# A graph network's second table stored as a float32r part and an exact rest, and summed with one float32r product a tile

## The reference, cut to what matters

```python
for l in range(2):
    W = jnp.einsum('rb,bio->rio', coeffs[l], bases[l])     # 8 relations, 256 x 256 each
    h = jnp.einsum('ni,rio->rno', x, W)                    # the table: node x relation -> 256 numbers
    msg = h[edge_type, src] * deg_inv[dst][:, None]        # one row of the table per edge
    agg = jax.ops.segment_sum(msg, dst, num_segments=6250)
    x_new = agg + x @ self_loops[l]
    x = relu(x_new) if l == 0 else x_new
# then: x_in + x + attention(xn), and experts on its layernorm
```

## Time and profile before

| | us |
|---|---|
| median of 3 runs | 2587.59 |
| lowest and highest run | 2583.8, 2588.66 |
| span of the profiled execution, first to last instruction | 3411.3 |
| POOL busy, idle before its gathers (profiled) | 1649.4, 1418.2 |
| PE busy, DVE busy, ACT busy (profiled) | 2398.6, 1074.1, 626.8 |

### The profile page before, as it was taken

The page is one execution under the profiler, slowest core; times in us unless marked ns, Lnnn a source line. Parts: engine busy times, 40 slices in busy tenths (PEclk is TensorE's granted clock), DMA queues, the critical chain, the costliest instruction groups (busy, mean ns, idle before and its releaser), DMA issues. The chain is left out here.

```text
span 3411.3 us, 37691 instructions
## 1 busy us (share of the span) xinstructions
PE 2398.6 (70%) x9525; PEld 1737.8 (51%) x9528; DVE 1074.1 (31%) x3125; ACT 626.8 (18%) x1391; POOL 1649.4 (48%) x1712
## 2 busy tenths in 40 slices
PE   6999357777777777776882766666666666566287
PEld 3788235555555555554561544444444444455065
DVE  3787022222222222222220333333233333234233
ACT  4455101111111111110120011111111211110033
POOL 0000655555555555555506555555655555551645
PEclk9999678888888888888895877777777777788587
DMA  8764433334333333433423332333332223231531
GB/s 225 250 232 192 139 100 123 128 125 133 123 124 124 126 124 125 128 122 112 131 90 93 88 91 87 88 87 88 91 88 84 86 87 90 85 87 32 164 110 54
DMA packets 159887, 397.24 MB, mean 116 GB/s; under 512 B 34926, under 2 KB 92241, under 8 KB 145932
## 3 DMA queue, kind: packets, MB, share of 16 engines
q0 software_dynamic: 81648, 219.65, 22.1%
q10 hardware_dynamic: 35772, 124.12, 9.4%
q1 hardware_dynamic: 42337, 51.93, 5.5%
HBM read 260.70 MB, written 138.94 MB: 117 GB/s over the span
## 5 line engine op out<-in xcount | busy, mean ns | idle before, releaser
L515 POOL DMA_INDIRECT gnn_ring<-table,g_idx x1564 | 1512.7, 967 | 1418.2 <-PE gnn_pagg L558 680.0
L558 PE MATMUL gnn_pagg<-gnn_ring,gnn_oh 128*128 x3904 | 1215.4, 460 | 483.7 <-issue 427.0
L558 PEld LDWEIGHTS gnn_pagg<-gnn_ring,gnn_oh 128*128 128x128 f32 x3904 | 838.0, 228 | 886.9 <-issue 759.7
L542 DVE TENSOR_TENSOR gnn_oh<-gnn_col,g_dst 128x256 f32<-128x256 f32 x976 | 408.9, 426 | 1471.2 <-DVEq L49 1214.0
L800 ACT COPY second_wr<-gnn_pm 128x512 f32<-128x512 f32 x196 | 103.0, 597 | 1107.8 <-DMA pre_bs<-in_L_gnn_bases 992.7
L1054 ACT ACTIVATE gnn_qe<-gnn_pq,gnn_bq 128x128 f32<-128x128 f32 x98 | 36.1, 368 | 1078.0 <-remote 1036.1
L402 PE MATMUL pre_psum<-pre_whigh,pre_high 128*128 128x512 f32 x392 | 159.0, 406 | 13.1 <-DVE pre_low L309 8.1
L336 DVE SCALAR_TENSOR_TENSOR second_wr<-pre_bs,pre_cr,second_wr 128x512 f32<-128x512 f32 x232 | 159.5, 748 | 2.8
L744 PE MATMUL gnn_pm<-gnn_whigh,gnn_high 128*128 128x512 f32 x392 | 157.5, 402 | 3.5 <-issue 2.5
L744 PE MATMUL gnn_pm<-gnn_whigh,gnn_low 128*128 128x512 f32 x392 | 153.8, 392 | 6.8 <-issue 6.7
L744 PE MATMUL gnn_pm<-gnn_wlow,gnn_high 128*128 128x512 f32 x392 | 152.9, 390 | 4.2 <-issue 4.2
(11 more groups left out here) (174 smaller groups left out, 2382.6 us busy)
## 6 DMA issues: line engine op xcount, KB each, us to landing
table<-pre_rows ACTq DMA_DIRECT2D x49, 1024.0 KB
table<-second_wr ACTq DMA_DIRECT2D x48, 1024.0 KB
gnn_ring<-table,g_idx POOLq DMA_INDIRECT x1564
bucket<-gnn_zrow SPq DMA_DIRECT2D x16, 650.0 KB
g_xT<-bucket SPq DMA_DIRECT2D x20, 520.0 KB, 6.3
pre_bs<-in_L_gnn_bases SPq DMA_DIRECT2D x32, 240.0 KB
pre_bs<-in_L_gnn_bases SPq DMA_DIRECT2D x30, 256.0 KB
x1T<-gnn_x1T ACTq DMA_DIRECT2D x49, 128.0 KB
```

Source lines behind the costliest of these rows:

```text
L515: eng.indirect_dma_start(self.ring[:, q % RG, t, 0:D], None, self.g.table[self.l][:, :], bass.IndirectOffsetOnAxis(ap=self.g.idx[:, at:at ...
L542: self.nc.vector.tensor_tensor(self.oh[:, h, :, :], self.col[:, :].unsqueeze(1).to_broadcast([P, n, P]), self.g.dst[:, ds(q * TPG + h * n, ...
L558: mm = nc.tensor.matmul(pagg[:, k, 0:self.width], self.oh[:, h, i, :], self.ring[:, ds(q & (RG - 1), 1), t, 0:self.width].rearrange("p o n ...
```

## The change

The second layer's table gets rows of 512 numbers (2 KB): the float32r part of the 256 numbers and, behind it, the rest (number minus part), which is stored as float32r as well. The second layer's sum multiplies such a row by a float32r matrix of ones and zeros, 512 columns in one product, and the two halves of the result are added afterwards. The ring of the second layer has 8 groups in place of 16, of 2 KB rows. In the first layer ACT's copy of a chunk writes the float32r part, DVE makes the rest of each chunk (`rows_low`, at the end of its step), and the block is stored with four DMAs of 512 KB, each after its rest is there; the buffer of a chunk is single. TensorE's next `multiply` waits for the four rests.

```diff
-RG = 16
+RG = (16, 8)
...
-        self.table = [dram(f"table{l}", (NP * R, D), F32) for l in range(2)]
+        self.table = [dram(f"table{l}", (NP * R, (1 + l) * D), F32) for l in range(2)]
...
+        self.rg = RG[l]
+        self.row = D if l == 0 else 2 * D
-        self.width = D + 1 if l == 0 else D
-        self.ring = s.sb("ring", [P, RG, TPG, ROW])
+        self.width = D + 1 if l == 0 else 2 * D
+        self.ring = s.sb("ring", [P, self.rg, TPG, ROW if l == 0 else 2 * D])
-        self.oh = s.sb("oh", [P, HALF, TPG // HALF, P])
+        self.oh = s.sb("oh", [P, HALF, TPG // HALF, P], F32 if l == 0 else F32R)
+        self.tiles = self.ring if l == 0 else self.ring[:, :, :, :].bitcast(F32R)
...
-                eng.indirect_dma_start(self.ring[:, q % RG, t, 0:D], None, self.g.table[self.l][:, :],
+                eng.indirect_dma_start(self.ring[:, q % rg, t, 0:self.row], None, self.g.table[self.l][:, :],
...
                     mm = nc.tensor.matmul(pagg[:, k, 0:self.width], self.oh[:, h, i, :],
-                                          self.ring[:, ds(q & (RG - 1), 1), t, 0:self.width].rearrange("p o n -> p (o n)"),
+                                          self.tiles[:, ds(q & (self.rg - 1), 1), t, 0:self.width].rearrange("p o n -> p (o n)"),
...
-        rows = wr
+        rows = wr[:, :, :].rearrange("p a (n r i d) -> p (a n) r i d", n=NC // 2, r=R // NC, i=2)
...
+            def rows_low():
+                for n in range(NC):
+                    reach(eng, hi_ok)
+                    V.tensor_tensor(rows[:, n, :, 1, :].bitcast(F32R), pm[:, n, 0:CW].rearrange("p (r d) -> p r d", d=D),
+                                    rows[:, n, :, 0, :], ALU.subtract).then_inc(lo_ok, 1)
+
             def step(b, k, prev):
                 agg.onehots(eng, b, seq)
...
                 front(k)
                 if b == NB - 1:
                     low_part(k)
+                if prev:
+                    rows_low()
...
             keys((NB - 1) % 2)
+            rows_low()
...
                 if b:
-                    eng.wait_ge(rows_ok, b)
+                    eng.wait_ge(lo_ok, NC * b)
...
-            def store(b, k):
-                reach(eng, stored[k], 16)
+            def store(b):
                 for n in range(NC):
+                    reach(eng, stored[n], 16)
                     reach(eng, chunk_ok)
-                    ins = nc.scalar.copy(rows[:, k, n * CW:(n + 1) * CW], pm[:, n, 0:CW])
-                    if b == NB - 1 and n == NC // 2 - 1:
-                        ins.then_inc(half_ok, 1)
-                        reach(eng, half_ok)
-                        eng.dma_start(table_rows(g, 1, b)[:, 0:R * D // 2], rows[:, k, 0:R * D // 2]).then_inc(stored[k], 16)
-                ins.then_inc(rows_ok, 1)
-                reach(eng, rows_ok)
-                lo = R * D // 2 if b == NB - 1 else 0
-                eng.dma_start(table_rows(g, 1, b)[:, lo:], rows[:, k, lo:]).then_inc(stored[k], 16)
+                    nc.scalar.copy(rows[:, n, :, 0, :].bitcast(F32R),
+                                   pm[:, n, 0:CW].rearrange("p (r d) -> p r d", d=D)).then_inc(hi_ok, 1)
+                for n in range(NC):
+                    reach(eng, lo_ok)
+                    eng.dma_start(table_rows(g, 1, b)[:, n * 2 * CW:(n + 1) * 2 * CW],
+                                  rows[:, n, :, :, :].rearrange("p r i d -> p (r i d)")).then_inc(stored[n], 16)
...
-                    ins = V.tensor_tensor(xb[:, j, :], xb[:, j, :], bo[:, :], ALU.add)
+                    V.scalar_tensor_tensor(out=xb[:, j, :], in0=agg.pagg[:, j, 0:D], scalar=g.dinv[:, ds(n - 1, 1)],
+                                           in1=xb[:, j, :], op0=ALU.mult, op1=ALU.add)
+                    ins = V.scalar_tensor_tensor(out=xl[:, :], in0=agg.pagg[:, j, D:2 * D], scalar=g.dinv[:, ds(n - 1, 1)],
+                                                 in1=bo[:, :], op0=ALU.mult, op1=ALU.add)
...
-                    ins = V.scalar_tensor_tensor(out=xb[:, j, :], in0=agg.pagg[:, j, 0:D], scalar=g.dinv[:, ds(n - 1, 1)],
-                                                 in1=xb[:, j, :], op0=ALU.mult, op1=ALU.add)
+                    eng.sem_inc(agg.agg_free, 1)
+                    ins = V.tensor_tensor(xb[:, j, :], xb[:, j, :], xl[:, :], ALU.add)
```

More of the change, by code:

```diff
@@ L29 @@
 NTP = NG * TPG
-RG = 16
+RG = (16, 8)
+REUSED = NG - min(RG)
 FREE = 2
@@ L85, in __init__ @@
         self.bound = s.sb("bound", [1, P], I32)
-        self.reuse = s.sb("reuse", [1, NG - RG], I32)
+        self.reuse = s.sb("reuse", [1, REUSED], I32)
         self.iota = s.sb("iota", [P, P])
@@ L160, in startup @@
         bni = s.sb("bni", [P, NB + 1], I32)
-        uio = s.sb("uio", [1, NG - RG], I32)
-        ush = s.sb("ush", [1, NG - RG], I32)
+        uio = s.sb("uio", [1, REUSED], I32)
+        ush = s.sb("ush", [1, REUSED], I32)
         idi = s.sb("idi", [P, P], I32)
@@ L488, in __init__ @@
         self.groups_in, self.gate, self.ring_ok = sems["groups_in"], sems["gate"], sems["ring_ok"]
-        self.landed = [s.sem(f"landed{j}") for j in range(RG)]
+        self.landed = [s.sem(f"landed{j}") for j in range(self.rg)]
         self.agg_ok, self.agg_free = sems["agg_ok"], sems["agg_free"]
@@ L499, in count @@
     def count(self, eng, between=None):
+        rg = self.rg
         for q in range(NG):
-            eng.wait_ge(self.landed[q % RG], 16 * sum(min(TPG, NT - p * TPG) for p in range(q % RG, q + 1, RG)))
+            eng.wait_ge(self.landed[q % rg], 16 * sum(min(TPG, NT - p * TPG) for p in range(q % rg, q + 1, rg)))
             eng.sem_inc(self.groups_in, 1)
@@ L507, in gather @@
     def gather(self, eng):
+        rg = self.rg
         for q in range(NG):
-            if q >= RG and q % FREE == 0:
-                last = eng.value_load(self.g.reuse[0:1, q + FREE - 1 - RG:q + FREE - RG], min_val=2, max_val=NG + NB)
+            if q >= rg and q % FREE == 0:
+                last = eng.value_load(self.g.reuse[0:1, q + FREE - 1 - rg:q + FREE - rg], min_val=2, max_val=NG + NB)
                 eng.wait_ge(self.pairs, last)
@@ L524, in begin @@
         if self.l == 0:
-            for j in range(RG):
+            for j in range(self.rg):
                 ins = self.nc.vector.memset(self.ring[:, j, :, D:ROW], 1.0)
@@ L602, in gnn_first @@
         xn_ok, xT_ps, high_ok, low_ok, split_ok = (s.sem(n) for n in ("xn_ok", "xT_ps", "high_ok", "low_ok", "split_ok"))
-        chunk_ok, half_ok, rows_ok = (s.sem(n) for n in ("chunk_ok", "half_ok", "rows_ok"))
+        chunk_ok, hi_ok, lo_ok = (s.sem(n) for n in ("chunk_ok", "hi_ok", "lo_ok"))
         p_ok, p_free, kt_ok, er_ok, kf_ok, kv_done = (s.sem(n) for n in (
@@ L607, in gnn_first @@
         kept = [s.sem(f"kept{k}") for k in range(2)]
-        stored = [s.sem(f"stored{k}") for k in range(2)]
+        stored = [s.sem(f"stored{n}") for n in range(NC)]
         dve_own = g.dve_own
@@ L821, in step @@
                 if prev:
-                    store(b - 1, 1 - k)
+                    store(b - 1)
                 reach(eng, kt_ok)
@@ L825, in step @@
                 nc.scalar.activation(kr[:, k, :], kt[:, k, :], ACT.Relu).then_inc(er_ok, 1)
+            for n in range(NC):
+                eng.sem_inc(stored[n], 16)
             for k in range(2):
-                eng.sem_inc(stored[k], 16)
                 eng.sem_inc(kept[k], 16)
@@ L833, in _ @@
                 step(b, b % 2, b > 0)
-            store(NB - 1, (NB - 1) % 2)
+            store(NB - 1)
+            for n in range(NC):
+                reach(eng, stored[n], 16)
             for k in range(2):
-                reach(eng, stored[k], 32 if k == (NB - 1) % 2 else 16)
                 reach(eng, kept[k], 16)
@@ L852, in gnn_second @@
         xb = s.sb("xb", [P, 2, D])
+        xl = s.sb("xl", [P, D])
         xf = s.sb("xf", [P, 2, D])
```

7 lines of the change are left out of this document (3 added, 4 removed).

## The result

The kernel before takes 2587.49 us (4 runs, 2583.8 to 2588.66), the changed one 2752.45 us (4 runs, 2749.94 to 2758.38): **slower by 165 us, ratio 1.0648, 95% interval 1.0633 to 1.0664**. It lies in the range, 42 us above the predicted 2710. The profiled execution of the changed kernel took 2749.94 us, with a span of 2748.2, so that its rows show the time of a plain run.

A forecast was written before the change was run, and what follows sets the result against it. The prediction took POOL's gathers to set the pace of both layers. Late rests 62, clock 53 and first layer's end 7 made 122 us on the median of 2587.6: 2710 us, range 2635 to 2760 us.

The forecast's parts named there:

- What bounds the kernel: Both layers: POOL's gathers, 1.267 us each, set the pace; the stretches sum to 2591 us against a median of 2587.6.
- The second layer at nothing: Second layer's sum: TensorE saves 293 us, none on the path, since POOL still issues 782 gathers; cost nothing.
- the 2 KB rows at nothing: Second layer's gathers: 2 KB rows may take the same 0.95 us, DMA share 0.40 to 0.80; no cost.
- The rests: First layer: subtractions delay the next one-hot matrices, sum 2.45 us late in 47 steps, 115 us less 53: 62 us.
- slack: First layer: TensorE alone needs 962 us, POOL's way 1014 us, leaving 53 us, 1.1 us a block.
- then 0.55 us idle: First layer, DVE: idle time put between the fourth subtraction's end and the one-hot comparison column, 0.55 us.
- The clock: First layer, TensorE: the clock falls after the wait in two blocks of three, 1.7 us each: 53 us.
- every block: Rival for the first layer: the clock falls in every block, 80 us, total 2737 us; chance 0.18.
- The first layer's end: End of the first layer: later last multiply, one more subtraction and 2 MB to store instead of 0.5 MB: 7 us.
- Transfers bound the second layer: Rival: a 2 KB row takes three times a 1 KB row, second layer 198 us longer, 2908 us; chance 0.04.
- not slower: Rival: POOL hides the late first-layer matrices and the second layer gives something back, 2564 us; chance 0.10.
- No fall: Rival for the first layer: the wait is too short for the clock to fall, 2657 us; chance 0.27.

The follow-up runs named there:

- Late rests: The changed kernel, with DVE making the rests of block b-2 behind the one-hot matrices of block b and ACT storing a step later: 2604.15 us.
- the traffic alone: The kernel before, with each 1 KB table row stored twice, gathered as 2 KB into a ring of 8 groups, float32 sum of the first half: 2603.74 us.
- stores_later_again: Second run of the changed kernel with ACT issuing a block's four stores one step later, DVE's order unchanged: 2711.43 us.
- the wait alone: The kernel before, with DVE waiting for ACT's four copies at the end of its first-layer step and nothing else changed: 2722.69 us.
- loads_first_again: Second run of the changed kernel with the next block's register loads and comparison column made before the four subtractions: 2606.55 us.

## Why the prediction was right, and where its sizes were off

**What bounds the kernel** held: the sum of 2591 us built from the rows of a disturbed profile against its own span of 3411.3. Each layer was right within 3 us; the stretch behind the first scatter was taken 10 us too long (199.1, measured 189.4). What I took for the profiling was a condition of the job; the sum tests only that the plain runs are free of it, and that is all the prediction used.

**The second layer at nothing, the 2 KB rows at nothing** held: 1022.8 and 1024.2 us, gathers of 967 ns, DMA share 0.75. Late rests and the traffic alone bound what the bytes cost over the whole kernel at 16 to 20 us, of which 14 and 12 lie in the two layers.

**The rests** held as a mechanism and were too small as a term. The prediction had the sum 2.45 us late in 47 steps, 115 us, less a slack of 53: 62. Measured is 155 - 8 = 147 us of lateness. The step that was off is "then 0.55 us idle": it is 1.06 in the block shown and 1.24 at the median, since the two register loads ahead of `col` take 0.45 and 0.70 us at the median where they took 0.30 each. The row of before from which the 0.55 came had no burst of stores beside it. The chain was also put together wrongly, which did not show in its size: it adds the subtraction (0.7) and the idle time (0.55), 1.25 us from the fourth copy to `col`, but the sequencer begins its loads with the subtraction. What lies there without a burst is the sequencer's work alone, 1.28 us in stores_later_again. That the two are equal is luck, and both expectations that took 0.7 us off for a missing subtraction (the rests left out, the wait alone) missed, in part at least, by it.

The slack was 43 us: 1176.1 less 147, 51 (clock) and 4 (end) leaves 974 us for TensorE alone, where 962 were forecast, and 1017.2 - 974 = 43. Two kernels test the 974 on their own. The loads ahead of the subtractions: 974 + 54 + 4 = 1032 us, measured 1392.68 - 358.49 = 1034. The wait alone, with 36 falls of the clock at 1.3 us and the layer's end as before: 974 + 129 + 47 = 1150, measured 1511.88 - 362.22 = 1149.7. So the term is 147 - 43 = 104 in place of 62. Two slips of the prediction's own sums are small beside that: its terms give a slack of 52, not 53, and an upper end of 2765, not 2760.

In stores_later_again, where the burst is elsewhere, lateness is 2.53 us and the time 2711.43, near the forecast of 2710. That kernel has the undisturbed loads that the chain was worked out with, but its time agrees in part by luck: there the rests make 121 - 43 = 78 us in place of 62 and the clock some 38 in place of 53.

**The clock** was 53 us and measures 48 to 50, if composed differently: falls of 1.3 us in 38 of 47 blocks, not of 1.7 in two of three. The 1.7 was half of the 3.4 us at half clock. But a product takes 0.435 us there and not twice the 0.26 of full clock, so that a fall costs 3.4 x (1 - 0.26 / 0.435) = 1.4 us. The rival "every block" would have put 80 us here. The Trainium skill (TensorE: Matmul & The Clock Gate, section HAM oscillation) has each step start cold where a long wait lies between the products of every step. The change's trace agrees for the most part, in 38 of 47 blocks; in loads_first_again, after 1.16 us of lateness, no block behind the first two is slow, and at 2.53 us 29 of 47 are.

**The first layer's end** was 7 us and is 4.4: from the end of the last sum 1535.16 - 1511.83 = 23.3 us against 18.95. The terms of that 7 were not measured one by one.

Together 104 + 51 + 4 = 159 us in the first layer, the 974 being chosen so, against a forecast of 122. The time lies 8 us under the upper end of a range 125 us wide; the forecast itself is 42 us short of 165.

**The rivals.** "Transfers bound the second layer" and "not slower" are out. "No fall" (2657) is out, since the clock fell in 38 of 47 blocks. "Every block falls" (2737) comes nearest in time, by a clock term that is too large and a lateness that is too small. The chance of 0.90 for slower rested on the late sum, and that was the right place.

None of the eight changed kernels beats the one before. The gathers, whose number none of them changes, bound both layers: 782 of 1.267 us in each. The best forms of the change, the rests moved behind the sum's matrices or the loads moved before the rests, come to within 16 to 20 us of it.

## What to carry to other kernels

Making the engine cheaper that doesn't set the pace brings nothing, and what feeds it can cost: before splitting a table for TensorE, count the gathers. Work that is appended to an engine's step is cheap only if nobody waits for what stands behind it in the same queue; look up what the next step begins with, and put that (register loads, small constants, the first matrices) ahead of the wait. Where a wait of two or three microseconds is opened in front of TensorE's products in each step, count the stretch at half clock beside it.

## What the runs showed of the hardware

- **Register loads from SBUF are slowed by a burst of stores.** DVE's second load of a block took 0.30 us, and 0.69 to 1.03 us (medians) while 2 MB were being stored, with a DMA share near 1; one of 1.21 us was seen (late_rests). With 1 MB stored by one DMA (the wait alone) it was 0.54 us. In the second layer, at a share of 0.75, it was 0.30 us.
- **A register load runs beside the operation issued before it.** It began at 1004.01 us, where the subtraction ran from 1004.00 to 1004.69; taking the subtraction out gained nothing.
- **A fall of the clock costs less than half of its length here.** A float32 product of the sum started each 0.26 us at 2.4 GHz and each 0.435 at 1.2; a stretch of some 3 us cost 1.3 us.
- **ACT's DMA issues back to back** get longer: four of 512 KB took 2.94 us in the block shown, and at the first layer's end 0.33, 0.44, 0.79 and 1.21 us one by one, where a lone one takes 0.33. ACT's next operation began 2.42 us after its last copy.
- **A 2 KB row costs POOL what a 1 KB row costs**: 966 ns for 128 of them, 964 for 1 KB rows (second layer). They land 3.7 us after the issue (median), rows of 1 KB after 2.8.
- **Whole jobs can have TensorE late at taking its instructions up**, 32% longer in all for this kernel (3423.54 against 2587.49 us, one job). A change must be compared with the kernel before in the same job, and a gain that only TensorE's side has (65 us here) shows only there. Why TensorE is late in such a job is open.
